# Cross-attention with two context branches: ScalarE does both direct heads before the subtracted heads' exponentials, VectorE writes the attention's low part last

## The reference

```
q = heads(x @ Wq.T)
text   = softmax(q k^T / sqrt(32)) v          k, v from the first 77 rows by Wk, Wv
second = softmax(q k_ip^T / sqrt(32)) v_ip    k_ip, v_ip from the last 77 by Wk_ip, Wv_ip
y = (text + second) @ Wo.T + bo + x
```

## Time and profile before

| | us |
|---|---|
| median of three runs | 534.23 (532.84 to 534.46) |
| the profiled execution | 537.34 |
| its span | 535.5 |

### The profile page before, as it was taken

How to read it: one execution, slowest core, us unless ns; L and a number is a source line. 1 busy time by engine, 2 the same in 40 slices (tenths; PEclk the granted TensorE clock), 3 DMA queues, 4 the chain that set the end, 5 groups by cost and what they waited for, 6 DMA issues and landing times.

```text
span 535.5 us, 16124 instructions
## 1 busy us (share of the span) xinstructions
PE 500.8 (94%) x5314; PEld 423.0 (79%) x5314; DVE 418.9 (78%) x654; ACT 372.4 (70%) x1690; POOL 306.7 (57%) x315
## 2 busy tenths in 40 slices
PE   8999676789999999999999999999999999999786
PEld 7999565568887888878888888888878888778565
DVE  0023778989998989989899898998989989888812
ACT  0145557678787887878878788888887878777610
POOL 2031415655766767666666675757677676654520
PEclk9999778989999999999999999999999999999999
DMA  8993228888999999999999999999999999989992
GB/s 301 413 353 158 69 87 239 288 250 267 305 292 282 303 311 293 309 292 304 306 291 306 299 304 306 291 306 298 302 306 290 307 299 296 296 282 301 295 273 74
DMA packets 104431, 149.17 MB, mean 279 GB/s; under 512 B 11728, under 2 KB 91088, under 8 KB 104144
## 3 DMA queue, kind: packets, MB, share of 16 engines
q1 hardware_dynamic: 104400, 148.77, 91.5%
HBM read 85.81 MB, written 62.91 MB: 278 GB/s over the span
## 4 chain that ended last, share of the span: by engine, by line
issue 34%; POOL 32%; PE 19%; DMA 5%; DVE 4%; SPq 2%; ACT 2%; POOLq 1%; DVEq 0%
POOL probs L356 16%; POOL x_lo L347 8%; POOL res L362 8%; PE q_ps L628 4%; PE s_ps L755 3%; PE pv_ps L665 2%; PE x_ps L628 2%; DMA y_out<-res 2%; PE pv_ps L755 2%; PE s_ps L653 2%; DMA p_last<-bounce_d 2%; DVE wo_lo L520 2%; SPq L295 1%; PE v_ps L755 1%; DVE row_neg L528 1%
## 5 line engine op out<-in xcount | busy, mean ns | idle before, releaser
L356 POOL TENSOR_TENSOR probs<-probs,row_inv 128x616 f32<-128x616 f32 x160 | 195.0, 1240 | 162.5 <-DVE row_inv L560 162.5
L399 ACT ACTIVATE probs<-s_ps,row_neg 128x77 f32<-128x77 f32 x640 | 198.8, 326 | 81.1 <-DVE row_neg L528 81.1
L528 DVE TENSOR_REDUCE row_neg<-s_ps 128x8 f32<-128x616 f32 x160 | 120.4, 794 | 45.0 <-PE s_ps L653 45.0
L399 ACT ACTIVATION_READ_ACCUMULATOR probs<-s_ps,row_neg 128x1 f32 x640 | 132.4, 207 | 0.0
L548 DVE STREAM_TRANSPOSE turned<-probs 128x512 f32<-128x512 f32 (+1 forms) x160 | 124.9, 818 | 1.8 <-POOL probs L356 1.8
L628 PEld LDWEIGHTS q_ps<-x_hi,wq_hi 128*128 128x128 f32 x400 | 59.4, 193 | 31.6 <-issue 31.6
L628 PE MATMUL q_ps<-x_hi,wq_hi 128*128 128x256 f32 x400 | 83.4, 306 | 0.0
L653 PE MATMUL s_ps<-keys,q 32*128 32x154 f32 x1280 | 65.5, 317 | 17.4 <-ACT probs L399 8.4
L628 PE MATMUL q_ps<-x_hi,wq_lo 128*128 128x256 f32 x400 | 74.4, 284 | 0.0
L628 PE MATMUL q_ps<-x_lo,wq_hi 128*128 128x256 f32 x400 | 74.1, 283 | 0.0
L653 PEld LDWEIGHTS s_ps<-keys,q 32*128 32x128 f32 x1280 | 48.8, 187 | 31.1 <-issue 30.7
(11 more groups left out here) (71 smaller groups left out, 610.8 us busy)
## 6 DMA issues: line engine op xcount, KB each, us to landing
bounce_d<-turned SPq DMA_DIRECT2D x80, 640.0 KB, 5.8
p_main<-bounce_d SPq DMA_DIRECT2D x320, 128.0 KB
res<-x_in SPq DMA_DIRECT2D x75, 128.0 KB, 5.0
y_out<-res SPq DMA_DIRECT2D x75, 128.0 KB, 4.8
x_raw<-x_in SPq DMA_DIRECT2D x70, 128.0 KB, 4.9
p_last<-bounce_d SPq DMA_DIRECT2D x80, 104.0 KB
stage<-wk_in SPq DMA_DIRECT2D x6, 640.0 KB, 7.5
stage<-wv_in SPq DMA_DIRECT2D x6, 640.0 KB, 10.6
```

Source lines behind the costliest of these rows:

```text
L356: nc.gpsimd.tensor_tensor(rows[:, :, keys], rows[:, :, keys], row_inv[:, u.slot, :, br].unsqueeze(2) .broadcast_to([P, GROUP * SUB, size]) ...
L399: done = nc.scalar.activation(rows[:, cols], s_ps[:, j, cols], ACT.Exp, bias=row_neg[:, j, i:i + 1], accum_out=row_sum[:, j, i:i + 1])
L528: nc.vector.tensor_reduce(row_neg[:, heads_of(half)], by_row(s_ps[:, heads_of(half), 0:SUB * BLK]), AXIS.X, ALU.max, negate=True).then_inc ...
```

## The change

On ScalarE both direct heads now come first, then the exponential of the subtracted heads, then the attention's high part. On VectorE the attention's low part is moved behind the row sums and the reciprocals, to the end of the unit. No instruction is added or taken away.

```diff
             def exps(u):
-                exp_direct(u, range(0, 1))
+                exp_direct(u, range(PAIR))
                 exp(u)
                 if u.plus(-VALUE_LAG).exists():
                     attn_high(u.plus(-VALUE_LAG))
-                exp_direct(u, range(1, PAIR))
...
                 if u.plus(-1).exists():
                     for part in range(BRANCHES):
                         turn(u.plus(-1), part)
+                invert(u)
                 if u.plus(-VALUE_LAG).exists():
                     attn_low(u.plus(-VALUE_LAG))
-                invert(u)
```

## The result

The changed kernel takes 547.4 us (546.05 to 548.47), the kernel before 534.35: the ratio is 1.0226, 95% interval 1.0185 to 1.0267. One of the four executions of the kernel before took 689.91 us and doesn't enter the ratio, which is not the quotient of the two medians (1.024). I had forecast slower, and 540.5; the time lies outside my range, 537 to 543.5.

A forecast was written before the change was run, and what follows sets the result against it. The round scores, maxima, direct heads, scores set the 5.55 us period, PE alone (5.46) and DMA close behind. +10.1-0.8-0.25-2.5-0.2 = +6.3 on the median 534.2 gave 540.5 us, range 537 to 543.5.

The forecast's parts named there:

- The mechanism: Later low part holds next unit's attention and, one unit in five, the group-0 chunk's last matmul; S is the scores' start.
- The group-0 chunk's last step: PE, units with g = 4: last matmul waits for the low part from S+5.25 to S+6.29, some 14 times.
- what the change gives back: Gains: -2.5 us before unit 10, -0.8 in units 75 to 78, -0.25 at unit 78, -0.2 in the tail.
- the price of the held step: Units 10 to 75, 13 tiles: 28.56 us per five units instead of 27.76, in all +10.1 us.
- the -0.8: Units 75 to 78: 17.33 us with one DMA wait before, 16.5 after.
- the 0.6 of longer periods of before: Units 10 to 75: of 1.0 us in longer periods, 0.4 was DMA in unit 73; 0.6 stay.
- Held attention: PE: next unit's attention starts 0.05 us behind the low part, at S+6.29; by itself a period of 5.52.
- DMA as a floor: SyncE's load issues advance 5.58 us a unit, taken as a limit on any faster pace.
- rival B: Low part ready in time, group-0 chunk not held; PE's 5.46 rules but DMA's 5.58 takes it back: 532, chance 0.06.
- Rival A: The stall is real and the rest dearer: 13.3 us in place of 10.1, less early gain: 545, chance 0.15.
- three conditions: Low part at its upper end (S+6.32), early gain under 1 us, PE's clock falling to 1.2 GHz in the stalls.
- Rival C: The stall only uses room PE had, DMA-bound time being hidden before: +0 to 1 us, 534.5, chance 0.09.

The follow-up runs named there:

- The runs with one unit in five: Changed kernel with high part before exponential, low part before sums in g = 4 units: 530.89 us; kernel before with both engines' new order there: 551.17.
- second trace: The kernel before, unchanged, run and traced again: 535.45 us (ratio 1.0006); its traced execution took 534.4, span 532.6.
- the run with the high part early: Against the kernel before: ScalarE does both direct heads, high part, then exponential; VectorE keeps its old order: 526.79 us (ratio 0.9836).
- the late order in g = 4: The kernel before, with the new order on ScalarE and VectorE only in units with g = 4: 551.17 us (ratio 1.0294).
- the other three runs: High part before exponential, VectorE's old order: 526.79 us; changed kernel with old-style early order in g = 4: 530.89; changed kernel with two attention PSUM banks: 542.07.

## Why the prediction was wrong
**The mechanism held.** The row sums, the reciprocals and the low part are where I had put them: reciprocals at S+5.73 (forecast 5.66), end of the low part S+6.26 (6.24), high part S+5.14 (5.09). VectorE overlaps its instructions by 0.08 as in the rows (315.25+0.25 against 315.42). The group-0 chunk's last step waits 15 times. Its start moves by 1.07, from S+5.25 to S+6.32; the list has only 0.6 of idle time for each, not the 1.0 that I had announced, because the record of the matmul before runs on to S+5.70. Step 12 waits for the high part, as foreseen inside the longer wait: it starts at S+5.20 instead of 5.01. Periods alternate in the other units; direct_done no longer sets the pace; the attention's waits for DMA are gone. The runs with one unit in five show that the held chunk makes the change a loss, and that the later exponential doesn't. What failed are sizes in the sum: what the change gives back, and the price of the held step with what goes along with it.

**The first term that failed: what the change gives back.** I took -2.5 ahead of unit 10, against one execution in which unit 10 started at 116.53. In its second trace it starts at 114.08: the gain is 0.3 to 0.9. The time that I worked out for unit 10 in the changed kernel, 113.1, was right (113.1 and 113.8); the start to which I compared it was not. The DMA waits, 0.4 in unit 73 and most of the -0.8, were of that execution too. I had the warning in the rows: its own time is 3.1 us above the median of the runs, and I carried its difference to that median as if the 3.1 had no place in it. That is 2.2 us ahead of unit 10 and 0.5 in the 13 tiles, of the 6.3 by which the forecast falls short in span. Behind unit 75 the forecast, -1.25 for -1.8, is near by luck: the -0.8 for units 75 to 78 are -0.1 against the second trace (16.65 and 16.55), and the rest of the tail gives more than I took.

**The second: the price of the held step.** +14.8 in 13 tiles where I had +10.1. Its parts, from the timeline of the changed kernel:
- Held matmul to scores: 0.32, not 0.21. I had read the 0.21 from a unit in which the last matmuls ran one behind the other. One that waits is recorded as 0.38 long instead of 0.28, and its weight load starts with it (both at 315.84), not 0.1 ahead as in front of a matmul that doesn't wait. 13 x 0.11 = 1.4. The low part's release is 0.03 later than I had it, 6.32 for 6.29: 0.4.
- The turn of the hardware loop falls on units 19, 29, 39, 49 and 59, all of them g = 4. There the held matmul is followed by scores only 0.60 later:

```profile
171.07 0.39 PE L627 MATMUL x_ps<-attn_lo,wo_hi 128*128 128x256 f32 x1 [0.62 <-DVE attn_lo L563]
171.67 0.54 PE L652 MATMUL s_ps<-keys,q 32*128 32x154 f32 x8 [0.21 <-issue]
```

  In the kernel before the turn cost 0.06 to 0.10 a time. I read it as hidden behind the wait for direct_done; where no engine holds TensorE, in the run with the high part early, it costs about 0.2. Now it is 0.26 to 0.30 more than a stall alone, 1.4 in all. I had carried over the 0.6 of longer periods of before: 0.8 short.
- Held attention: it starts 0.05 to 0.16 behind the low part (once 0.21), where I had 0.05 throughout, and so as late as S+1.01 and not 0.82. So the four other units take 22.0 to 22.3, not 22.06; 1.5 in 13 tiles.

These come to 4.1; with the 0.5 of above they are the difference of 4.7, but for rounding.

**The third: DMA as a floor.** It didn't enter the forecast, but it held rival B at 532. B's mechanism, the low part in time, was run, by another order: 526.8. SyncE's rate of 5.58 was that of a queue which followed a pace of 5.55 (5.54 in the second trace), with slack that changes slowly, and not a ceiling. That PE alone needs 5.46 was right; the measured mean is 27.3 / 5.

Rival A would have given 545, nearer than my forecast, and one of its three conditions came true, an early gain under 1. The low part did not end at its upper bound (S+6.26, not 6.32), so A's 13.3 for the tiles is near the 14.8 by luck, and TensorE's clock did not fall in the stalls. The granted clock of the changed kernel, from its page, answers to the earlier trace rows:

```profile
PEclk9999988999999999999999999999999999999999
```

Rival C, a stall inside hidden time, is out: in the second trace of the kernel before there is no DMA-bound time.

What stays open is why the first trace was 2.4 us late ahead of unit 10. Two units hold it: unit 1 is 1.2 longer than in the second trace and unit 9 1.4 (6.96 against 5.55), both with a stretch of TensorE at 1.2 GHz in them (mean granted clock 0.69 and 0.75); the first unit starts 0.4 earlier. The traces differ in such stretches in a way that I haven't tested. Both traces of the kernel before and the runs with ScalarE's order alone, VectorE's order alone and the late order in g = 4 have one between 103 and 114 us; both traces of the changed kernel and the other three runs have none from 90 us to 500. So a part of what the changed kernel gains ahead of unit 10 may be the clock.

## What to carry to other kernels
Follow each moved instruction to every place that waits for it, and look above all at waits that are met with little to spare and so appear in no list: here 0.26 us of room in one unit of five decided, and an order that keeps the low part in time (high part before the exponential, low part before the sums) turns the same idea into a gain of 1.6%. Price a released wait from a row where that instruction really waited, and add what the old wait had covered, the turn of a loop too. A profiled execution that lies above the median contains something of its own; find it before its parts become gains.

## What was not expected of the hardware
A matmul that waits cost more than the wait: 0.38 instead of 0.28 us, and scores 0.32 instead of 0.21 behind its start. SyncE's steady rate near the kernel's own period (5.58 against 5.55) was not its limit; in the faster kernel it ran at 5.46. The turn of the hardware loop cost TensorE 0.06 to 0.10 us where ScalarE set the pace and 0.26 to 0.30 behind a held matmul.
